# Sub-experts: half of the gates arrive by repeated reads from memory, and GpSimd takes a quarter of the products; the embedding is loaded and moved in smaller parts

## The reference, cut to what matters

```python
    # embedding: a 16x16 convolution plus a position, then the text rows behind it
    patches = lax.conv_general_dilated(pixel_values, conv_w, window_strides=(PATCH, PATCH), ...)
    h = jnp.concatenate([h, txt], axis=1)
...
    # sub-experts: S=8 groups, R=16, M=64 experts in a group, K=4 chosen, H=32 hidden, G=64
    z = jnp.einsum('nd,sdr->nsr', xf, P)
    scores = jnp.einsum('nsr,smr->nsm', z, C)
    topv, topi = jax.lax.top_k(scores, K)
    w = jax.nn.softmax(topv, axis=-1)
    h = jax.nn.gelu(jnp.einsum('nsr,nskrh->nskh', z, W1g) + b1g)
    yl = jnp.einsum('nskh,nskhr->nskr', h, W2g) + b2g
    comb = jnp.einsum('nskr,nsk->nsr', yl, w)
    out = jax.nn.gelu(comb @ G1 + g1b) @ G2 + g2b
```

## Time and profile before

| | us |
|---|---|
| median of 3 runs | 2085.52 (2079.92 to 2085.99) |
| the profiled execution, its own time | 2105.55 |
| its span, first to last instruction | 2103.8 |
| PE busy | 1833.3 (87%) |
| DVE busy | 1217.4 (58%) |
| ACT busy | 837.3 (40%) |
| POOL busy | 379.6 (18%) |

### The profile page before, as it was taken

One profiled execution on the slowest core, in us unless ns is written; L12 is line 12 of the kernel. 1 busy time (PEld: TensorE's weight loads), 2 busy tenths in 40 slices (PEclk: granted clock), 3 DMA queues, 4 the chain that ended last, 5 costly groups with the idle time before them and its releaser, 6 DMA issues. The chain is left out here.

```text
span 2103.8 us, 38744 instructions
## 1 busy us (share of the span) xinstructions
PE 1833.3 (87%) x13908; PEld 1329.7 (63%) x14000; DVE 1217.4 (58%) x3641; ACT 837.3 (40%) x1667; POOL 379.6 (18%) x380
## 2 busy tenths in 40 slices
PE   6889969977885999778888875999999999979997
PEld 4678759966664799567655542333333588647886
DVE  2478842238998222467635554788888567792221
ACT  1155423314551111235425455667677354311111
POOL 1100111242311331431001111000000000223543
PEclk9999879998995899879999877899999999999999
DMA  5000345510004555102000014900000000304662
GB/s 201 1 1 0 124 136 187 181 52 15 12 0 142 176 180 158 29 19 86 0 1 17 28 48 128 290 27 1 1 1 1 24 1 0 133 19 126 191 178 64
DMA packets 83839, 156.75 MB, mean 75 GB/s; under 512 B 22390, under 2 KB 57942, under 8 KB 82806
## 3 DMA queue, kind: packets, MB, share of 16 engines
q1 hardware_dynamic: 63669, 134.71, 19.6%
q0 software_dynamic: 19552, 19.63, 3.9%
q10 hardware_dynamic: 480, 0.63, 0.1%
HBM read 125.04 MB, written 29.48 MB: 73 GB/s over the span
## 5 line engine op out<-in xcount | busy, mean ns | idle before, releaser
L2390 DVE TENSOR_TENSOR l2s_gated<-l2s_hidden,ps 128x408 f32<-128x408 f32 x512 | 262.7, 574 | 58.6 <-PE ps L2293 58.3
L2360 ACT ACTIVATE l2s_hidden<-ps,pack_l2f 128x816 f32<-128x816 f32 x256 | 227.2, 938 | 98.2 <-PE ps L2285 97.5
L130 PE MATMUL ps<-pack_const 128*128 128x512 bf16 x496 | 150.2, 438 | 36.5 <-PEq L164 9.4
L2293 PE MATMUL ps<-l2s_gs,l2s_spread 96*128 96x408 bf16 x512 | 150.8, 341 | 0.3 <-DVE l2s_gated L2390 0.3
L2285 PE MATMUL ps<-l2s_zs,l2s_up 128*128 128x408 bf16 x512 | 133.0, 342 | 14.4 <-DMA l2s_gs<-g_parts 14.4
L1903 PE MATMUL ps<-l_down,l_hidden 128*128 x792 | 139.8, 326 | 0.0
L1903 PEld LDWEIGHTS ps<-l_down,l_hidden 128*128 128x128 f32 x792 | 127.3, 190 | 0.4
L130 PEld LDWEIGHTS ps<-pack_const 128*128 128x128 bf16 x588 | 59.7, 109 | 97.2 <-issue 60.1
L2305 PE MATMUL ps<-l2s_gated,l2s_down 128*32 128x408 f32 x1024 | 114.3, 518 | 4.0 <-DVE l2s_comb L2377 3.7
L2285 PEld LDWEIGHTS ps<-l2s_zs,l2s_up 128*128 128x128 bf16 x512 | 39.7, 97 | 119.4 <-ACT l2s_hidden L2360 82.2
L1862 POOL DMA_INDIRECT l_xt<-rows_in,l_tokens x66 | 63.2, 958 | 255.5 <-PE ps L1875 196.3
(11 more groups left out here) (468 smaller groups left out, 3943.2 us busy)
## 6 DMA issues: line engine op xcount, KB each, us to landing
l_up<-in_l_up SPq DMA_DIRECT2D x66, 576.0 KB
l3c_wg<-in_l_gate SPq DMA_DIRECT2D x16, 576.0 KB
l3c_wu<-in_l_up SPq DMA_DIRECT2D x16, 576.0 KB
l3c_wd<-in_l_down SPq DMA_DIRECT2D x16, 576.0 KB
slots_out<-l_y SPq DMA_DIRECT2D x66, 96.0 KB
l_down<-in_l_down SPq DMA_DIRECT2D x8, 675.0 KB, 9.4
g_parts<-l2b_g_parts SPq DMA_DIRECT2D x12, 408.0 KB, 4.1
l_down<-in_l_down SPq DMA_DIRECT2D x8, 576.0 KB, 7.1
```

What stands on the lines that cost most here:

```text
L130: pe.matmul(bank, halves[:, 0:128], halves[:, :], start=True, stop=True)
L2293: pe.matmul(gate_bank(n), spread[:, t % 8, :], gs[half][2 * r + odd][:, t // 8, pair, chunk(n % 2), :], start=True, stop=True).then_inc(ga ...
L2360: act.activation(hidden[:, p % kept, :, :], ps[:, 0, 2 * (p % 2):2 * (p % 2) + 2, 0:NG], ACT.Gelu_apprx_tanh, bias=w.at("b1")[:, s * MT + ...
L2390: dve.tensor_tensor(gated[:, n % ring, :], hidden[:, n // 2 % kept, n % 2, :], gate_bank(n), ALU.mult)\
```

## The change

**Embedding.** `tok_pack` is loaded in seven transfers (weights and patches of two steps `k` each, three times, then the positions), and TensorE starts when the first two are there; its loop runs over `k` outside and over the chunks inside. The 16 moves into `h` are issued half by SP and half by ACT. The six packs for later phases are issued in `retention`.

**Gates.** Of the four column blocks, only blocks 0 and 2 are split into three bf16 parts (the instructions of lines 1455, 1614, 1464 and 1167 work on 204 columns in place of 408); blocks 1 and 3 are stored as they are, in f32, into a new tensor `g_whole`. `gT` gets two buffers. Each chunk of four samples has a fourth store.

**Sub-experts.** The order of the 128 hidden values of a tile is turned round (32 outside, 4 experts inside). For `pair` 0 the gates are spread by TensorE as before; for `pair` 1 a transfer reads the four rows of `g_whole` 32 times into all 128 partitions (`whole`, six buffers, 3,264 bytes a row, one transfer for each group, issued by SP when the group six before is consumed). In each group DVE multiplies three chunks and GpSimd the fourth. `kept` grows from 3 to 4, `ring` shrinks from 10 to 8.

```diff
@@ embed
+            for k in range(CONV_K // 2):
+                for first, cols in ((first_w, 2 * D), (first_x, 2 * B * NP)):
+                    there = slice(first + k * cols, first + (k + 1) * cols)
+                    sp.dma_start(pack[:, there], dram["pack_tok"][:, there]).then_inc(weights_loaded[k], 16)
+            sp.dma_start(pack[:, first_place:], dram["pack_tok"][:, first_place:]).then_inc(places_loaded, 16)
...
             for q in range(G):
-                sp.wait_ge(emb_ready, q + 1)
-                for j in range(GB):
-                    sp.dma_start(g["h"][0:NP, q * GB + j, :], emb[j * NP:(j + 1) * NP, q, :]).then_inc(moved, 16)
-            for name in PACKS:
-                if name not in ("tok",) + FIRST + LATE:
-                    sp.dma_start(g["pack_" + name][:, :], dram["pack_" + name]).then_inc(g["packs_loaded"], 16)
+                moves(sp, q, 0)
...
+        @block.scalar
+        def _(act):
+            for q in range(G):
+                moves(act, q, 2)
@@ fusion_and_gates
+                sp.dma_start(g["g_whole"][:, :, there, :], gT[:, c % 2, 1:4:2, :, :]).then_inc(g_stored[c % 2], 16)
...
-                    act.activation(g_parts[:, n // GB % 2, 0, :, n % GB, :], gT_view, ACT.Copy)
-                    if n >= GB and n % GB == 0:
-                        act.wait_ge(b2_ps, 2 * (n // GB))
-                    act.activation(gT[:, :, n % GB, :], gT_view, ACT.Copy).then_inc(gT_ready, 1)
+                    act.activation(g_parts[:, n // GB % 2, 0, :, n % GB, :], gT_split, ACT.Copy)
+                    if n >= 2 * GB and n % GB == 0:
+                        act.wait_ge(b2_ps, 2 * (n // GB - 1))
+                    act.activation(gT[:, n // GB % 2, :, n % GB, :], gT_view, ACT.Copy).then_inc(gT_ready, 1)
@@ sub_experts
-    gates, kept, group, ring = 3, 3, 4, 10
+    gates, kept, group, ring, ahead = 3, 4, 4, 8, 6
...
+            def whole_gates(n):
+
+                half, r, odd, t, _ = order[2 * n]
+                row = 64 * odd + 4 * t
+                if n >= ahead:
+                    sp.wait_ge(gated_ready, 3 * (n - ahead + 1))
+                    sp.wait_ge(late_ready, n - ahead + 1)
+                sp.dma_start(whole[:, n % ahead, :, :].rearrange("p c n -> p (c n)"),
+                             g["g_whole"][row:row + 4, r, half * HALF:(half + 1) * HALF, :]
+                             .rearrange("e b l -> e (b l)").unsqueeze(0).broadcast_to([32, 4, HALF * L]))\
+                  .then_inc(whole_loaded[n % ahead], 16)
...
+            for k in range(4):
+                parts(0, k)
+                up_weights(k)
+                if k:
+                    gate_parts(sp, 0, k)
+                else:
+                    for n in range(ahead):
+                        whole_gates(n)
+                down_weights(k)
...
+            for n in range(ahead, groups):
+                if n % 8 == 0 and 2 <= n // 8 < 6:
+                    parts(1, n // 8 - 2)
+                    gate_parts(sp, 1, n // 8 - 2)
+                whole_gates(n)
...
+                if p % 2 == 0:
+                    gates_spread(p // 2)
+                elif p >= 3:
+                    second(p // 2 - 1)
...
+        @block.gpsimd
+        def _(pool):
+            for n in range(groups):
+                pool.wait_ge(gate_ps, 2 * n + 1)
+                pool.wait_ge(whole_loaded[n % ahead], 16 * (n // ahead + 1))
+                pool.wait_ge(hid_ready, 2 * n + 2)
+                pool.tensor_tensor(gated[:, (4 * n + 3) % ring, :], hidden[:, (2 * n + 1) % kept, 1, :],
+                                   whole[:, n % ahead, 1, :], ALU.mult).then_inc(late_ready, 1)
...
-            for n in range(2 * pairs):
...
+            for n in range(groups):
+                dve.wait_ge(hid_ready, 2 * n + 1)
+                for c in range(2):
+                    dve.wait_ge(gate_ps, 2 * n + c + 1)
+                    dve.tensor_tensor(gated[:, (4 * n + c) % ring, :], hidden[:, 2 * n % kept, c, :], gate_bank(2 * n + c),
+                                      ALU.mult).then_inc(gated_ready, 1)
...
+                dve.wait_ge(whole_loaded[n % ahead], 16 * (n // ahead + 1))
+                dve.wait_ge(hid_ready, 2 * n + 2)
+                dve.tensor_tensor(gated[:, (4 * n + 2) % ring, :], hidden[:, (2 * n + 1) % kept, 0, :],
+                                  whole[:, n % ahead, 0, :], ALU.mult).then_inc(gated_ready, 1)
```

More of the change, by code:

```diff
@@ L1269, in bias_products @@
                     row = 64 * (c % 2) + HP * r
[L1270 removed]
+                    last = pe.matmul(gT_bank[row:row + HP], wf.at("b2", RG)[:, 2 * half + r, :], gT[:, c % 2, 2 * half + r, :, :],
                                      start=True, stop=True)
@@ L2196, in sub_experts @@
         zs = [[m.sb(f"zs{half}{k}", [128, 2, HALF, L], BF16) for k in range(4)] for half in range(2)]
-        gs = [[m.sb(f"gs{half}{k}", [96, 2, 2, HALF, L], BF16) for k in range(4)] for half in range(2)]
+        gs = [[m.sb(f"gs{half}{k}", [96, 2, HALF, L], BF16) for k in range(4)] for half in range(2)]
+        whole = m.sb("whole", [128, ahead, 2, NG])
         comb = m.sb("comb", [128, 2, 2, GB, L])
@@ L2289, in gates_spread @@
             def gates_spread(n):
-                half, r, odd, t, pair = order[n // 2]
-                if n >= gates:
-                    pe.wait_ge(gated_ready, n - gates + 1)
-                pe.matmul(gate_bank(n), spread[:, t % 8, :], gs[half][2 * r + odd][:, t // 8, pair, chunk(n % 2), :],
-                          start=True, stop=True).then_inc(gate_ps, 1)
-            def second(n):
-                if n % per_sum_bank == 0 and n:
-                    pe.wait_ge(comb_ready, n // per_sum_bank)
-                pe.wait_ge(gated_ready, n + group)
-                for at in range(n, n + group):
-                    half, r, odd, t, pair = order[at // 2]
-                    if not half and t == 0 and pair == 0 and at % 2 == 0:
-                        pe.wait_ge(down_loaded[2 * r + odd], 16)
-                    row = HP * (2 * (at % 2) + pair)
-                    last = pe.matmul(sums[row:row + HP, :], down[2 * r + odd][:, pair, t, :], gated[:, at % ring, :],
-                                     start=(odd == 0 and t == 0), stop=(odd == 1 and t == MT - 1))
-                if (n + group) % per_sum_bank == 0:
+                half, r, odd, t, _ = order[2 * n]
@@ new lines, in gates_spread @@
+                for c in range(2):
+                    j = 2 * n + c
+                    if j >= gates:
+                        pe.wait_ge(gated_ready, 3 * ((j - gates) // 2) + (j - gates) % 2 + 1)
+                    pe.matmul(gate_bank(j), spread[:, t % 8, :], gs[half][2 * r + odd][:, t // 8, chunk(c), :],
+                              start=True, stop=True).then_inc(gate_ps, 1)
+            def second(n):
+                half, r, odd, t, _ = order[2 * n]
+                if n % in_bank == 0 and n:
+                    pe.wait_ge(comb_ready, n // in_bank)
+                pe.wait_ge(gated_ready, 3 * (n + 1))
+                pe.wait_ge(late_ready, n + 1)
+                if not half and t == 0:
+                    pe.wait_ge(down_loaded[2 * r + odd], 16)
+                for pair in range(2):
+                    for c in range(2):
+                        row = HP * (2 * c + pair)
+                        last = pe.matmul(sums[row:row + HP, :], down[2 * r + odd][:, pair, t, :],
+                                         gated[:, (4 * n + 2 * pair + c) % ring, :],
+                                         start=(odd == 0 and t == 0), stop=(odd == 1 and t == MT - 1))
+                if (n + 1) % in_bank == 0:
@@ L2335, in _ @@
                     up_products(p + 1)
-                for n in (2 * p, 2 * p + 1):
-                    gates_spread(n)
-                if p >= 3 and p % 2 == 1:
-                    second(2 * p - 6)
-            second(2 * pairs - group)
+                if p % 2 == 0:
+                    gates_spread(p // 2)
+                elif p >= 3:
+                    second(p // 2 - 1)
+            second(groups - 1)
             fill(pe, g, ps[:, 0, 2, :], 8)
```

107 lines of the change are left out of this document (54 added, 53 removed).

## The result

| | before | after |
|---|---|---|
| median on one chip | 2085.76 us (4 runs) | 2039.11 us (4 runs: 2036.49 to 2042.18) |
| ratio, 95% interval | | 0.9779 [0.9759, 0.9799] |
| span of the profiled execution | 2103.8 us | 2038.6 us |

The account below looks back on a forecast made before the run. No engine was full: the sub-experts' loop was a circle of spread products awaiting gate banks and DVE awaiting spread products. Terms -32.7 - 5.5 - 4 = -42 us took 2085.5 to 2043; range 2014 to 2076, forecast's own 2028 to 2062.

Parts of the forecast that it names:

- The loop: Sub-experts: 2.0 us a group instead of 2.46, DVE's third product held 0.44 us behind GpSimd's; phase -32.7 us.
- The first `second`: Sub-experts' start: six `whole` transfers go ahead of the first `down`, so the first `second` starts at 1328.3.
- half clock: Sub-experts, after the pause: granted clock starts at half for about 4 us, costing 2 us.
- The pause: Sub-experts, seventh group: TensorE, ACT and DVE stand still about 17 us while SP's queue works off 8.6 MB of loads.
- The takeovers of the sums: Sub-experts, mid-loop: DVE takes over the sums three times, 2.1 us each, say 7 in all.
- The floor of 1.87 us: Sub-experts, one group: lower bound from TensorE's work, 3 x 0.35 + 0.82 us.
- no lock: Sub-experts: GpSimd and DVE share SBUF without loss, group 1.87, 16 us more gain, 2027; chance 0.2 together with no pause.
- The transfers: Sub-experts: a `whole` of 0.418 MB takes 1.3 us (320 GB/s; bounds 1.05 to 1.96) and hides under a group.
- The rival in which they bound the loop: Sub-experts: at 213 GB/s a `whole` takes 1.96 us, some 2.1 us a group; 2060, up to 2079; chance 0.16.
- the slower one: Sub-experts: 32 repetitions reading the same four rows hinder each other; at 2.6 us a transfer 2132; chance 0.11.
- The embedding: Program start: smaller first loads and moves on two queues start the next phase earlier, -5.5 us (bounds -3 to -7).
- The gates: Gates' phase, 16 samples: shorter ACT copy and DVE subtraction, 6.6 us at most, -4 taken.

Follow-up runs that it names:

- no_meeting: Changed kernel with DVE's third product taking its gate from a PSUM bank instead of `whole` in SBUF; ratio to the kernel before 0.9733.
- late_second: Changed kernel with `second` issued one group later, gated ring 8 to 12, sums taken over behind the third product; ratio to the kernel before 0.9724.
- four_outside: Changed kernel with each `whole` transfer written as four rows outside, 32 repetitions inside; 2326.86 us against 2103.39 before (one run).
- embed_only: Kernel before with only the embedding's part of the change; ratio to the kernel before 0.9961.
- spread_late: Changed kernel with SyncE's loads spread among the `whole` transfers and `second` one group later; 2008.43 us, ratio to the kernel before 0.9617.

## Why the prediction was right, and where it was not

- **The loop.** Forecast 291.2 us from the first product to the end of the last `second`, measured 291.3 (1286.4 to 1577.7), 31.5 less than before. The mechanism, GpSimd first and DVE's third product 0.44 us behind it, is shown by the rows above and by no_meeting (0.57 us without the meeting), and its price by late_second. But that the sum came out to 0.1 us is luck: up to the seventh `second` it has 41.4 us, and the trace 34.3 (1286.40 to 1320.66); from there to the end 249.8, and the trace 257.1. Two errors of 7 us offset each other.
- **What was too long in it.** The first `second` came 7.5 us after the start, not 9.3. From it, at 1293.94, to 1319.03 the 8.6 MB and the seventh `whole` (0.42) took 25.1 us, 360 GB/s and not 320, which is 3.2 us. The 2 us of half clock stood ahead of the seventh `second`; they came behind it. The pause itself was 12.5 to 14 us, not 17, by the faster queue and because the six groups ahead of it took 12.5 us and not 10.8, the first at half clock (0.64 at 1294:1297).
- **What was too short.** A group was 2.02 and not 2.0 (2.4 us over 121). The half clock behind the pause took 2.2 us in three steps (8.3 instead of 3 x 2.02). The takeovers of the sums cost 9.4 us and not 7.
- **The floor of 1.87 us** under a group was wrong: the step from bf16 `up` to f32 `second` is 0.44 and not 0.35 us, so the floor was 1.97. The forecast of 2.0 put the whole distance from 1.87 down to the meeting; only 0.06 of it was the meeting, and 0.09 TensorE's own step. The group came out right in part because the one error stood in for the other. So the gain of "no lock" was 0.06 us a group, some 7 us over 121 groups, and not the 16 that this rival was given. no_meeting and late_second, 8 and 10 us faster than the change by their ratios (0.9733 and 0.9724 against 0.9771), fit it within their intervals.
- **The takeover** of the sums: the wait was 2.1 us each, as forecast. But by GpSimd's starts the five long steps around the three takeovers are 9.4 us longer than 2.02 each, where the sum had 7. Behind two of them the clock fell to half (0.51 at 1445:1448), which the prediction did not have.
- **The transfers.** Over the loop the queues moved 229 GB/s at a share of 0.71, so a `whole` of 0.418 MB alone would take 1.3 us (an estimate: 0.418 / (229 / 0.71) = 1.30), as assumed. The rival in which they bound the loop fell, as did the slower one: the engines wait for a `whole` only at the pause. That 32 reads of the same rows don't hinder each other at all is not shown: at full share the steady loop's transfers would move 301 GB/s (202 / 0.67), those of four_outside 400 (104 / 0.26), and no run says why. The Trainium skill (DMA: Bandwidth & Descriptors, section Latency and other measured facts) has its 103 to 207 GB/s for copies between tensors in memory whose rows lie 512 KiB to 8 MiB apart, and calls the meeting on memory channels an inference. The rows of `g_whole` lie 13 KB apart, so those figures were no measure for this transfer, and no run here shows such a case. The 104 GB/s of four_outside come with a quarter of the engines.
- **The embedding** was undersized: -7.7 us in the trace and -8 in embed_only, not -5.5. The first loads were there at 4.67, not at 6, and TensorE's own work shrank to 9.68 from 10.64.
- **The gates** were undersized most: -4 forecast. From the first product of L1206 to the first `up`, the trace has 262.8 before and 250.8 after, 12.0 less: 5.6 to 6.9 for the narrow operations (the prediction's bound was 6.6), 2.0 for the shorter wait ahead of the first `up` (1.0 was forecast), and 3 to 4 not taken apart. DVE's longer waits, which I let swallow a third of the 6.6, swallowed little or nothing.
- **The sum.** By the traces -31.5 - 8 - 12 = -51.5; measured -46.7, by its interval -42 to -50. Forecast -42. The embedding and the gates made it more than forecast; the loop did not. The remaining few us lie within what the intervals and single profiled executions leave open.

The pause and its half clock were foreseen as a cost of the change, and they were its largest one: 21 of the 32 us that spread_late gained lay in the order of a queue.

## What to carry to other kernels

When small transfers with a deadline share a queue with large loads that have none, put the large ones between the small ones, each just ahead of its need; six small transfers ahead of the first `down`, and a block of 8.6 MB ahead of the seventh, cost 21 us here, the clock included. Before a stall of one engine is priced, add up the others' steps at their start-to-start distances, also where the kind of product changes: it set the floor of the group, and with it what removing the stall could give. Of the two orders of the broadcast tried here, the one with the long repetition (32) outermost kept the transfers hidden; the one with the four rows outermost made the kernel 11% slower than before. And look at the clock behind every short stop: a wait of 2.1 us was followed by some 3 us at half clock in two cases of three, and in spread_late, with 2.0, in none.

## What the runs showed that was not expected

- With the repetition of 32 outermost the transfers of the steady loop ran at 202 GB/s for a share of 0.67; with the four rows outermost they ran at 104 GB/s and a share of 0.26, for the same bytes.
- Of two products with both operands in SBUF, one on GpSimd and one on DVE, the one that started second was held, whichever it was: 1.13 instead of 0.57 us on DVE, 1.39 instead of 1.05 on GpSimd.
- The step from the bf16 product to the f32 product with 32 weight columns took 0.44 us start to start instead of 0.35, wherever nothing was waited for, and the trace before had it too.
- The same code took 15 to 21 us longer in attention of layer 2 on the slower chips, at a granted clock of 0.87 to 0.90 over the phase instead of 0.92 to 0.93. Spans of two executions are no measure of a change of this size.
